# Gated cross-attention and mixture-of-experts block: order of the last products and per-store waits at the border between attention and slot assignment

## The reference

```python
x = x + tanh(g_xattn[0]) * attention(layernorm(x), ctx_1024, ctx_1024, ctxb_2048x32, Wq, bq, ..., Wo, bo)
x = x + tanh(g_ffn[0]) * ffn(layernorm(x), router_w, wg_r, wu_r, wd_r, wg_s, wu_s, wd_s)
# ffn, on flat tokens:
gs = einsum('td,ndm->tnm', flat, wg_s); us = einsum('td,ndm->tnm', flat, wu_s)
out = einsum('tnm,nmd->td', silu(gs) * us, wd_s)
probs = softmax(flat @ router_w)
weights, indices = top_k(probs, 2)         # normalised, then spread over 16 experts
h = silu(g) * u * comb[:, :, None]         # g, u: routed gate and up products
out = out + einsum('tem,emd->td', h, wd_r)
```

## Time and profile before

| | us |
|---|---|
| median of 3 runs | 1949.95 |
| lowest and highest run | 1945.26, 1951.6 |
| the profiled execution, its own time | 1966.69 |
| its span, first to last instruction | 1964.9 |
| PE busy | 1884.7 (96%) |
| DVE, ACT, POOL busy | 1144.3, 876.2, 1226.0 |
| mean granted TensorE clock | 0.983 |

### The profile page before, as it was taken

One profiled execution on the slowest core, in us unless ns is written; L12 is line 12 of the kernel. 1 busy time (PEld: TensorE's weight loads), 2 busy tenths in 40 slices (PEclk: granted clock), 3 DMA queues, 4 the chain that ended last, 5 costly groups with the idle time before them and its releaser, 6 DMA issues. The chain is left out here.

```text
span 1964.9 us, 41718 instructions
## 1 busy us (share of the span) xinstructions
PE 1884.7 (96%) x13066; PEld 1534.8 (78%) x13067; DVE 1144.3 (58%) x1760; ACT 876.2 (45%) x1681; POOL 1226.0 (62%) x1368
## 2 busy tenths in 40 slices
PE   7799999999999999999999999999788999999898
PEld 6587887878788887878888787888567878888786
DVE  4666565756656575665657566565546733333467
ACT  3344454554445455444545544454442336666000
POOL 2377676877768677776867777686551524443472
PEclk9899999999999999999999999999898999999999
DMA  6855748475574947557484755748316365554796
GB/s 208 213 137 137 212 112 232 117 189 152 148 205 116 234 118 188 152 147 210 117 227 120 187 152 145 209 116 216 103 48 253 92 219 166 166 169 146 208 272 190
DMA packets 171271, 331.39 MB, mean 169 GB/s; under 512 B 20294, under 2 KB 69446, under 8 KB 170454
## 3 DMA queue, kind: packets, MB, share of 16 engines
q1 hardware_dynamic: 154460, 285.79, 52.2%
q0 software_dynamic: 10800, 33.30, 5.9%
q10 hardware_dynamic: 5968, 11.75, 1.7%
HBM read 214.44 MB, written 115.80 MB: 168 GB/s over the span
## 5 line engine op out<-in xcount | busy, mean ns | idle before, releaser
L989 DVE TENSOR_REDUCE neg_max<-score 112x1 f32<-112x750 f32 x508 | 476.4, 938 | 491.2 <-PE score L1324 490.4
L683 ACT ACTIVATE probs_t<-st_pair 125x448 f32<-125x448 f32 x768 | 416.7, 543 | 500.7 <-PE st_pair L1350 496.2
L547 POOL TENSOR_TENSOR acc<-acc,probs_t 125x448 f32<-125x448 f32 x256 | 325.0, 1270 | 51.8 <-ACT probs_t L683 51.4
L1281 PE MATMUL proj<-ctx_hi,weights 128*128 128x376 f32 (+1 forms) x1024 | 329.6, 347 | 2.1 <-DVE weights L1039 2.1
L549 POOL TENSOR_TENSOR acc<-acc,probs_t 125x448 f32<-125x448 f32 x256 | 302.6, 1182 | 20.1
L1350 PE MATMUL st_pair<-q_stack,k_stack 98*125 98x224 f32 x1536 | 312.7, 286 | 0.0
L1324 PE MATMUL score<-k_stack,q_stack 96*112 96x512 f32 x1016 | 276.9, 354 | 20.6 <-DVE neg_max L989 11.6
L1350 PEld LDWEIGHTS st_pair<-q_stack,k_stack 98*125 98x125 f32 x1536 | 266.2, 189 | 33.3 <-issue 1.3
L1291 PE MATMUL proj<-weights,ctx_hi 128*125 128x512 f32 x768 | 247.1, 403 | 0.0
L539 POOL TENSOR_TENSOR acc<-probs_t 125x448 f32<-125x448 f32 x128 | 147.1, 1150 | 158.5 <-PE pv L1403 143.4
L1281 PEld LDWEIGHTS proj<-ctx_hi,weights 128*128 128x128 f32 x1024 | 192.4, 190 | 28.1 <-issue 16.1
(11 more groups left out here) (259 smaller groups left out, 3089.8 us busy)
## 6 DMA issues: line engine op xcount, KB each, us to landing
k_stack<-k_parts SPq DMA_DIRECT2D x192, 375.0 KB, 6.3
k_parts<-k_hi SPq DMA_DIRECT2D x64, 375.0 KB, 6.7
k_parts<-k_lo SPq DMA_DIRECT2D x64, 375.0 KB, 7.2
ctx_raw<-in_ctx_t SPq DMA_DIRECT2D x62, 375.0 KB, 8.6
y_slots<-y_sb SPq DMA_DIRECT2D x71, 256.0 KB, 2.1
q_stack<-q_parts SPq DMA_DIRECT2D x64, 224.0 KB, 5.0
gu_sb<-in_w_gu ACTq DMA_DIRECT2D x4, 2048.0 KB, 15.1
x_in<-in_x SPq DMA_DIRECT2D x16, 448.0 KB, 9.3
```

The lines of the kernel that those rows point to most:

```text
L547: nc.gpsimd.tensor_tensor(both, both, tiles(c, p, pair, 0), ALU.add).then_inc(half_added, 1)
L683: act.activation(probs_t[0:KW, (c * PHASES + p) % 2, u % HC, :], st[u % 2][0:KW, 0:2 * L], ACT.Exp)\
L989: nc.vector.tensor_reduce(neg_max[:, h // HC % 2, h % HC, t:t + 1], score_place(b, h, t)[0:QW, 0:S], axis=AX.X, op=ALU.max, negate=True).t ...
L1281: ins = nc.tensor.matmul(bank[:, 0:w], wp[:, d, c * P:(c + 1) * P], xp[:, d, at:at + w], start=(d == 0 and k == 0), stop=(d == DC - 1 and ...
```

## The change

The fourth part of the down product, `down(3)`, is moved ahead of the last transposes on PE. The four waits at the end of SP's stream in the attention block are removed, and the four semaphores they looked at outlive that block. In the next block each transfer waits for what it reads, or for what has to be out of the memory that it writes: SP waits for the columns' stores and issues the column loads, then waits for the logits' stores and issues the logit load (the order of these two is exchanged), then waits for the stores into `x1` and issues the residual load. ACT waits for the stores into `x1` and `xn_rows` ahead of its four weight loads. POOL waits for the stores into `xn_rows` ahead of its gathers.

```diff
@@ attention_phase, SP, end of its stream
             store_cols(B - 1, B)
             store_logits(B - 1, B)
-            sp.wait_ge(x1_stored, (B + GT) * 16)
-            sp.wait_ge(rows_stored, B * 16)
-            sp.wait_ge(cols_stored, PRE["cols_stored"] + B * 16)
-            sp.wait_ge(logits_stored, PRE["logits_stored"] + B * 16)
@@ attention_phase, PE, end of its stream
-            for j in (1, 2):
+            for j in (1, 2, 3):
                 down(j)
             for t in range(QT):
                 turn_result(B - 1, t, B)
-            down(3)
             for t in range(QT):
                 route(t, B)
@@
+PRE = {"cols_stored": 16, "logits_stored": 16}
+X1_STORED, ROWS_STORED = 16 * (B + GT), 16 * B
+COLS_STORED, LOGITS_STORED = PRE["cols_stored"] + 16 * B, PRE["logits_stored"] + 16 * B
@@ head_and_slots, SP
+            sp.wait_ge(cols_stored, COLS_STORED)
+            load_columns(sp, xc, xn_cols, FIRST_IN_BLOCK + 1, columns_in)
+            sp.wait_ge(logits_stored, LOGITS_STORED)
             sp.dma_start(logit[:, :, :], logits).then_inc(logits_in, 16)
-            load_columns(sp, xc, xn_cols, FIRST_IN_BLOCK + 1, columns_in)
+            sp.wait_ge(x1_stored, X1_STORED)
             load_total(0)
@@ head_and_slots, POOL, behind the copy of the indices
             pool.wait_ge(index_ready, 1)
+            pool.wait_ge(rows_stored, ROWS_STORED)
             for k in range(ASTEP):
                 nc.gpsimd.indirect_dma_start(xg[:, k, :], None, xn_rows,
@@ head_and_slots, ACT, first lines
+            act.wait_ge(x1_stored, X1_STORED)
+            act.wait_ge(rows_stored, ROWS_STORED)
             for n in range(LOADS):
                 e = E_R // LOADS
                 each = DC * GATE_UP
@@ program: the four semaphores are made once, outside both blocks, and passed down
+        stores = [memory.enter_context(nc.semaphore(name))
+                  for name in ("x1_stored", "rows_stored", "cols_stored", "logits_stored")]
```

More of the change, by code:

```diff
@@ L85, in attention_phase @@
                     x1, xn_rows, xn_cols, logits, ws_gu, ws_d, g_ffn, weights, parts, shared,
-                    xc, xc_parts, tanh_g2):
+                    xc, xc_parts, tanh_g2, stores):
     q_dram = nc.dram_tensor("q_parts", (B, DC, HC, 2, DH, L), F32, kind="Internal").ap()
@@ L206, in attention_phase @@
         res_loaded = sem("res_loaded")
-        x1_stored = sem("x1_stored")
+        x1_stored, rows_stored, cols_stored, logits_stored = stores
         xn2_ready = sem("xn2_ready")
-        rows_stored = sem("rows_stored")
-        cols_stored = sem("cols_stored")
-        logits_stored = sem("logits_stored")
         stacked = [sem(f"stacked{c}") for c in range(DC)]
@@ L254, in attention_phase @@
         res_ready = sem("res_ready")
-        PRE = {"cols_stored": 16, "logits_stored": 16}
         STACK_SET = 16 * (3 + 2)
@@ L1778, with experts_phase @@
 FIRST_IN_BLOCK = 1
-def experts_phase(nc, x1, xn_rows, xn_cols, logits, w_gu, w_d, shared, xc, xc_parts, tanh_g2, out):
+PRE = {"cols_stored": 16, "logits_stored": 16}
+X1_STORED, ROWS_STORED = 16 * (B + GT), 16 * B
+COLS_STORED, LOGITS_STORED = PRE["cols_stored"] + 16 * B, PRE["logits_stored"] + 16 * B
+def experts_phase(nc, x1, xn_rows, xn_cols, logits, w_gu, w_d, shared, xc, xc_parts, tanh_g2, stores, out):
     y_slots = nc.dram_tensor("y_slots", (USED_TILES * P, D), F32, kind="Internal").ap()
@@ L1817, in experts_phase @@
                            tanh_g2, weight, slot_i, slot_token, tile_expert, prev_expert, xc, xc_parts, work,
-                           y_sb, total_stored, gather_at, xg, index_ready, gathered)
+                           y_sb, total_stored, gather_at, xg, index_ready, gathered, stores)
             routed_experts(nc, xn_rows, xn_cols, y_slots, gu_sb, d_sb, ident2, slot_token, tile_expert, prev_expert,
@@ L1857, in head_and_slots @@
                    tanh_g2, weight, slot_i, slot_token, tile_expert, prev_expert, xc, xc_parts, work,
-                   y_sb, total_stored, gather_at, xg, index_ready, gathered):
+                   y_sb, total_stored, gather_at, xg, index_ready, gathered, stores):
     es = ExitStack()
@@ L2857, in program @@
         attention_phase(nc, x, ctx_t, ctxb, g_xattn, wq, bq, wk, bk, wv, bv, wo, bo, router_w, x1, xn_rows, xn_cols, logits,
-                        ws_gu, ws_d, g_ffn, weights, parts, shared, xc, xc_parts, tanh_g2)
-        experts_phase(nc, x1, xn_rows, xn_cols, logits, w_gu, w_d, shared, xc, xc_parts, tanh_g2, out)
+                        ws_gu, ws_d, g_ffn, weights, parts, shared, xc, xc_parts, tanh_g2, stores)
+        experts_phase(nc, x1, xn_rows, xn_cols, logits, w_gu, w_d, shared, xc, xc_parts, tanh_g2, stores, out)
```

## The result

| | before | changed |
|---|---|---|
| median of 6 runs, us | 1951.2 | 1970.1 |
| lowest and highest | 1945.26, 1953.88 | 1968.16, 1976.06 |
| the profiled execution, its own time | 1966.69 | 1971.5 |
| its span | 1964.9 | 1969.8 |

The change makes the kernel slower: the ratio is 1.0096 with a 95% interval of 1.0074 to 1.0117, which is 18.9 us between the medians. The forecast was 1972.3.

A forecast was written before the change was run, and what follows sets the result against it. PE bounds the kernel, 96% busy, its border restart set by the logits' landing. Later logits, +20.4, and half-clock restart, +2.0, give +22.4 us on the median 1949.95: 1972.3; terms' bounds 1969 to 1976, widened by 3 each side, down to 1964.

The forecast's parts named there:

- PE's restart follows the landing of the logits by 4.0 us: At the block border, PE's next matmuls start 4.0 us after the logit load lands, so that landing sets the change's worth.
- Part 1, down(3): Before the last transposes: 12 matmuls fill PE's hole, route ends sooner and the logits' copy comes 4.2 us earlier.
- Part 2, the stores: SP's stores bunch 0.5 us apart: next block starts 6.8 us earlier, but x1 lands only at about 1482.0.
- Part 3, who loads first: Next block's loads: weights, columns, then logits; queues alternate packets one for one, so the logits land 20.4 us later.
- The rule of long turns: DMA engines switch queues every 9 to 17 descriptors, leaving logits little late; related rival +3.5 us, chance 3%.
- Part 4, the restart: Twelve matmuls behind the silu run at half clock after PE's long stand: +2.0 us, bounds 0 and 4.
- The columns did not win the race: Rival at the next block's loads: SP's loads served before weights, logits +0.1 us, time 1951; chance 9%.
- The rival as the edit reads: Border stores land at single latencies, logit load takes 3.4 us: logits 3.7 us sooner, time 1946.2; chance 3%.
- L: Landing time of the logit load in the next block, forecast at 1509.8 instead of 1489.4.

The follow-up runs named there:

- e4: Kernel before with only the two loads exchanged, columns ahead of logits; ratio 1.0125 (1.0082 to 1.0167), routed experts 22.6 us later than before.
- e7: Changed kernel with 115 extra matmuls filling PE's stand between first and second gate and up product; routed experts 20.5 us later than before.
- e3: Changed kernel with only the weight loads moved behind the first four silus, columns still ahead of logits; ratio 1.0002 (0.9977 to 1.0027) to before.
- e6: Changed kernel with the same weights in 16 loads of 4 KB rows instead of 4 of 16 KB; routed experts 16.0 us later than before.
- e2: Changed kernel with logits loaded ahead of columns and each weight load behind one of the first four silus; ratio 0.9997 (0.9974 to 1.0021) to before.
- e8: e2 plus the logits' store ahead of the columns' store, its load waiting for that store only; median 1945.0 against 1949.2, ratio 0.998 to before.
- e5: Kernel before with only down(3) moved ahead of the last transposes, block-end waits kept; single time 1946.84 against a median of 1949.2.
- e1: Changed kernel with SP's logit load put back ahead of the column loads, all waits kept; ratio 1.0038 (1.0014 to 1.0062) to before.
- e9: e2 with down(3) put back behind the last transposes; routed experts 1.7 us later than before.

## Why the prediction held

The forecast was the right mechanism, and its sum of +22.4 stands against +20.1 in the distances and +18.9 (14 to 23 by the interval) in the medians.

- **PE's restart follows the landing of the logits by 4.0 us.** Right: 3.98 or 3.99 in all eleven executions.
- **Part 1, down(3).** Right: route ran behind the transposes, and the copy of the logits came 4.0 us sooner against the normalisation; 4.2 was forecast. Both count from an execution in which `down(3)` ran at a clock of 0.61; against e4 it is 2.5. DVE's additions beside POOL's chain cost nothing that shows: the normalisation starts 7.33 us behind DVE's last `x_res<-proj` before and after.
- **Part 2, the stores.** The block was forecast 6.8 us sooner and came 5.1 us sooner. The step that was mis-sized is SP's spacing of 0.5 us: four stores took 2.68 us of issue and the columns 1.32. It had no weight, since ACT's issue of the weights hangs on the landing of x1. That was forecast for 1482.0, 8.0 us behind the normalisation's start, and ACT issued at 8.0.
- **Part 3, who loads first.** Right in each point: weights ahead of columns ahead of logits, turns one for one, landing behind the end of the weights. Its size was +20.4 and is +18.6. The logit load took 23.5 us where 25 were worked out. The difference is in the weights, at whose end the logits land: from their first issue to the last landing they took 23.4 us, and 25.2 in the execution of before that the forecast took over. The same order gave 24.2 in e4 and 25.0 in e7 for the logit load, so this is within what executions differ by. e4 shows that the order alone does it, e3 that it needs the weights beside it, and e6 that the turns count packets. The rule of long turns from the Trainium skill ("DMA: Bandwidth & Descriptors", queues, rings and completion order) does not agree with e6's 535 to 545 either. Equal counts over a long stretch could come of equally long turns of both queues as well, but the changed kernel's trace has 29 packets of q10 and 28 of q1 in the single microsecond from 1490 to 1491, where a weight row takes some 0.55 us of an engine: turns of nine such rows would last 5 us.
- **Part 4, the restart.** +2.0 was forecast; twelve matmuls took 4.13 us instead of 2.44, +1.7, and 1.6 from restart to routed experts. e7 shows that it is the clock.
- **The rivals.** The columns did not win the race, since they were issued 1.1 us behind the weights. The rival as the edit reads gave L 3.7 us sooner than before; the maximum of e2 comes 3.6 us sooner and that of e8 4.7. That its total agrees with e2 is partly luck: that rival had the logit load issued 8.2 us behind the normalisation's start and landing in 3.4, and in e2 it was issued at 9.4 and landed in 2.5, with the logits first and the weights late.

What the change does by parts, in the distance to the routed experts, each part added to the last: moving `down(3)` -2.4 (e5); removing the waits, with the logits still loaded first, +8.3 (e1 against e5); exchanging the two loads +14.2 (changed against e1); together +20.1. The middle part was not forecast by itself. It lets the block begin 2.9 us sooner, but the logit load, which still waits for the stores, goes out only 0.5 us sooner (9.27 instead of 9.73), while the weights go out 1.8 us sooner (7.96 instead of 9.74). So the weights are 1.3 us ahead, the load lands in 9.9 us instead of 3.4, and the restart falls to half clock. With the weights late it is -1.3 instead (e2 against e5): 0.4 us of that is the earlier issue of the logit load and 0.9 us its quicker landing. The waits themselves were thus worth next to nothing here. No run has early weights issued behind the logit load with the waits removed.

## What to carry to other kernels

When a wait at a block's end is taken away, look at what each queue issues first in the new order and at how long its rows are: small transfers that the next step needs have to stand ahead of small ones that it doesn't, and large rows on the other queue should start behind both. Price a short load by the packets ahead of it in its own queue times the other queue's packet time, not by bytes, and no further than the end of the other queue's work: in the changed kernel 71 turns of 0.55 us would be 39 us, but each engine had only 36 weight rows, and the load landed with their end after 23.5. The price was too low where it applied, 7.4 us against 9.9 (e1) and 16 against 18.0 (e6). A wait at a block's end may hold back a competitor more than it holds back the load that matters, as in e1 against e5. And work that PE does ahead of a wait gains nothing by coming sooner; it can lengthen the stand so that the restart is at half clock (e9).

## What was not expected

**The last block differs between executions, whatever the kernel.** From its first gate product to the span's end it took 143.2 us in the profiled execution of before, 128.1 in that of the changed kernel, 136 to 138 in e1 to e4 and e9, and 128.5 to 130 in e5 to e8. In the six long ones PE stands 5 to 12 times, for 0.15 to 1.75 us each and 4.1 to 7.2 us in all, with nothing that released it; in the five short ones never. In before that is 7.2 of the 15.1 us between it and the changed kernel; its granted clock over the block was 0.98 instead of 1.00. Three of the rows of before:

```profile
1842.11 0.37 PE L2783 MATMUL up_bank<-xc_parts,weights 128*128 128x448 f32 x1 [0.76 <-issue]
1843.53 0.46 PE L2783 MATMUL up_bank<-xc_parts,weights 128*128 128x448 f32 x1 [1.05 <-issue]
...
1845.64 0.53 PE L2783 MATMUL up_bank<-xc_parts,weights 128*128 128x448 f32 x1 [1.03 <-issue]
```

The cause is open. It is why distances to a point ahead of that block tell more here than spans.

**The issue of a store on SP is dearer behind others.** The store that is issued sixth in the bunch of seven took 1.1 to 1.35 us of SP's time in the changed kernel, e1 to e3 and e5 to e8, against 0.40 where the stores were spread (before), and the seventh 0.4 to 0.75 us. With the slower pace of the four ahead, that moved the block's start by 1.7 us, which was not in the forecast. Why the sixth is dear is not shown.

**Short stands ahead of the silu cost nothing, longer ones a product at or near half clock.** In e3 and e9, with 4.45 and 4.79 us, the twelve matmuls behind took 4.1 and 4.6 us; in the kernel before, e2, e5, e7 and e8, with 0.33, 1.94, 0.76, 1.31 and 1.20 us, they took 2.54 to 2.56.
